# Decay factors in a PSUM bank, one PSUM bank for the attention output

## What is computed

```python
def bi_wkv(r, k, v, w, u, time_emb):          # used twice, with r = x and k = v = f
    tf = sigmoid(sum(time_emb))
    decay = exp(-exp(w)) * (0.5 + 0.5 * tf)   # per channel and batch
    ek = exp(min(k, 30)); ekv = ek * v
    # a = a * decay + ekv, b = b * decay + ek, over the 256 tokens,
    # once forward (nf, df) and once in reverse (nb, db)
    euk = exp(min(u + k, 30))
    num = nf + nb - ekv + euk * v
    den = df + db - ek + euk
    return sigmoid(r) * num / max(den, 1e-8) * (0.8 + 0.2 * tf)

x = x + attention(bi_wkv(x, f, f, w1, u1, cond))    # 16 heads of 16
x = x + moe_ffn(bi_wkv(x, f, f, w2, u2, cond))      # 64 experts, 6 used, and 2 shared tiles
```

## Time and profile before

| | before |
|---|---|
| median of 3 runs | 434.53 us (433.73 to 434.86) |
| the profiled execution's own time | 433.69 us |
| its span in the profile | 431.9 us |
| TensorE busy (matmul) | 333.6 us, 77% |
| VectorE busy | 305.9 us, 71% |
| ScalarE busy | 186.8 us, 43% |
| GpSimd busy | 140.3 us, 32% |

### The profile page before, as it was taken

The page is one execution under the profiler, slowest core; times in us unless marked ns, Lnnn a source line. Parts: engine busy times, 40 slices in busy tenths (PEclk is TensorE's granted clock), DMA queues, the critical chain, the costliest instruction groups (busy, mean ns, idle before and its releaser), DMA issues.

```text
span 431.9 us, 6069 instructions
## 1 busy us (share of the span) xinstructions
PE 333.6 (77%) x1628; PEld 261.3 (60%) x1628; DVE 305.9 (71%) x658; ACT 186.8 (43%) x373; POOL 140.3 (32%) x123
## 2 busy tenths in 40 slices
PE   0014337747876786888857999999999999999995
PEld 0013225536654675665546788888888888888884
DVE  6999988995799866777567766556565565555654
ACT  4014030535261545557352555455554555545541
POOL 2608553325223002003303443443334433344331
PEclk9998555955895798899798999999999999999999
DMA  5940390850183039010100111111011101111102
GB/s 168 176 132 24 116 151 2 198 97 2 50 187 59 3 112 172 14 50 2 51 0 0 51 49 49 49 49 38 35 49 49 49 31 42 49 49 49 30 18 97
DMA packets 16947, 28.02 MB, mean 65 GB/s; under 512 B 2418, under 2 KB 10786, under 8 KB 15906
## 3 DMA queue, kind: packets, MB, share of 16 engines
q1 hardware_dynamic: 16930, 27.82, 27.7%
HBM read 20.81 MB, written 5.24 MB: 60 GB/s over the span
## 4 chain that ended last, share of the span: by engine, by line
issue 31%; DVE 13%; POOL 10%; PE 9%; ACT 3%; DMA 2%; POOLq 1%; DVEq 1%; SPq 0%; ACTq 0%
POOL scan L418 9%; DVE scan L1075 4%; PE ps L1182 2%; DVE mx L804 2%; DMA k_st<-qk_split 1%; PE ps L1150 1%; PE ps L1169 1%; PE ps L1212 1%; PE ps L1139 1%; ACT prob L495 1%; PE ps L1223 1%; DVE hid L850 1%; DMA qk_split<-qk_lo 0%; DVE scan L736 0%; ACT o_raw L502 0%
## 5 line engine op out<-in xcount | busy, mean ns | idle before, releaser
L418 POOL TENSOR_TENSOR scan<-scan 128x512 f32<-128x512 f32 x68 | 75.4, 1111 | 131.5 <-ACT scan L556 131.5
L1075 DVE TENSOR_TENSOR scan<-scan,ps 128x512 f32<-128x512 f32 x64 | 44.0, 687 | 60.0 <-POOL scan L418 60.0
L560 ACT ACTIVATE q_st<-scan 128x512 fp32r<-128x512 f32 x64 | 40.5, 632 | 58.8 <-PE ps L1286 52.2
L1266 PE MATMUL ps<-hid_hi,k_st 128*128 128x512 f32 (+1 forms) x140 | 55.0, 393 | 2.5 <-DVE k_st L960 2.2
L1150 PE MATMUL ps<-k_st,q_st 96*128 96x256 f32 x128 | 34.8, 394 | 27.1 <-DMA k_st<-qk_split 21.7
L1079 DVE TENSOR_TENSOR q_st<-scan,q_st 128x512 fp32r<-128x512 f32 x64 | 44.1, 689 | 16.3 <-ACT q_st L560 16.3
L556 ACT ACTIVATE scan<-ps 128x512 f32<-128x512 f32 x68 | 40.4, 598 | 33.5 <-PE ps L1268 31.6
L1284 PE MATMUL ps<-q_st,k_st 128*128 128x512 f32 x136 | 54.3, 399 | 0.6 <-POOL q_st L429 0.4
L1268 PE MATMUL ps<-hid_hi,k_st 128*128 128x512 f32 (+1 forms) x140 | 54.7, 391 | 0.0
L1267 PE MATMUL ps<-hid_lo,k_st 128*128 128x512 f32 (+1 forms) x140 | 54.6, 390 | 0.0
L1285 PE MATMUL ps<-q_st,k_st 128*128 128x512 f32 x136 | 53.9, 396 | 0.0
(11 more groups left out here) (133 smaller groups left out, 542.7 us busy)
## 6 DMA issues: line engine op xcount, KB each, us to landing
clip<-in_tiles SPq DMA_DIRECT2D x34, 256.0 KB, 2.6
q_st<-qk_split SPq DMA_DIRECT2D x16, 256.0 KB, 4.8
k_st<-qk_split SPq DMA_DIRECT2D x32, 128.0 KB, 5.5
qk_split<-qk_hi SPq DMA_DIRECT2D x8, 256.0 KB, 2.1
qk_split<-qk_lo SPq DMA_DIRECT2D x8, 256.0 KB, 2.1
f_sb<-in_fT SPq DMA_DIRECT2D x4, 256.0 KB, 10.1
x_sb<-in_xT SPq DMA_DIRECT2D x4, 256.0 KB, 9.2
out<-f_sb SPq DMA_DIRECT2D x4, 256.0 KB, 2.3
```

Source lines behind the costliest of these rows:

```text
L418: g.tensor_tensor(sq[:, half], relu[:, half], relu[:, half], ALU.mult).then_inc(sq_ready, 1)
L1075: TT(act[:, half], sq[:, half], bank_w(half), ALU.mult).then_inc(act_ready, 1)
L1266: mm(bank_h(slot)[:, cols], w_hi, x_hi, start=(c == 0), stop=False)
```

## The change

`decay` is no tensor in SBUF any more but the first 16 floats of PSUM bank 5 on every partition. The attention output has only bank 4. `values` waits for ScalarE's copy of the group before it (`o_raw_ready`), where it waited for that of the group before the last.

```diff
--- before.py
+++ after.py
@@ -89,7 +89,7 @@
         cfac = sb("cfac", [P, B])
         dexp = sb("dexp", [P, 2 * KC])
         dbase = sb("dbase", [P, 2 * KC])
-        decay = sb("decay", [P, 2 * KC, B])
+        decay = ps[:, 5, 0:2 * KC * B].rearrange("p (n b) -> p n b", b=B)
 
         clip = sb("clip", [P, 4, KC, S])
         gkv = clip[:, 0:2]
@@ -209,8 +209,8 @@
         def bank_t(n):
             return ps[:, 2 + n % 2, :].rearrange("p (t q) -> p t q", t=QT)
 
-        def bank_o(n):
-            return ps[:, 4 + n % 2, 0:S]
+        def bank_o():
+            return ps[:, 4, 0:S]
 
 
         jobs = [("q", 0), ("k", 0), ("v", 0)]
@@ -499,7 +499,7 @@
                 if b > 0:
                     n = job_no[("ot", b - 1, 1)]
                     sc.wait_ge(misc_full[n % 2], n // 2 + 1)
-                a.activation(o_raw[:, grp], bank_o(4 * b + grp), ACT.Copy).then_inc(o_raw_ready, 1)
+                a.activation(o_raw[:, grp], bank_o(), ACT.Copy).then_inc(o_raw_ready, 1)
 
             def evacuate_o_ch(b):
                 job_wait(sc, ("oc", b))
@@ -1172,14 +1172,14 @@
 
             def values(b, grp):
 
-                if 4 * b + grp > 1:
-                    pe.wait_ge(o_raw_ready, 4 * b + grp - 1)
+                if 4 * b + grp > 0:
+                    pe.wait_ge(o_raw_ready, 4 * b + grp)
                 pe.wait_ge(v_ready, QT * (b + 1))
                 pe.wait_ge(prob_ready, H * b + 4 * grp + 4)
                 for kt in range(QT):
                     for j in range(4):
                         h = 4 * grp + j
-                        last = mm(bank_o(4 * b + grp)[32 * j:32 * j + 32, :], v_aug[:, b % 2, kt, h, :],
+                        last = mm(bank_o()[32 * j:32 * j + 32, :], v_aug[:, b % 2, kt, h, :],
                                   prob[:, (H * b + h) % PRING, kt, :], start=(kt == 0), stop=(kt == QT - 1))
                 last.then_inc(pv_ready, 1)
```

## The result

| | before | after |
|---|---|---|
| median | 434.69 us (433.73 to 435.44, 4 runs) | 419.72 us (416.96 to 421.15, 4 runs) |
| profiled execution, its span | 433.69, 431.9 us | 419.32, 417.5 us |
| mean granted TensorE clock | 0.893 | 0.902 |

The ratio is 0.9649, 95% interval 0.9595 to 0.9703: 3.5% faster. I had predicted 419.

A forecast was written before the change was run, and what follows sets the result against it. VectorE's scans, taking turns with GpSimd on SBUF, were taken to bound the time before the expert tiles. Relief 16.1 less bank waits 1.05 gives 15.05 us; predicted 419 us (chance 0.74), range 415.5 to 424.5 for 8 in 10.

The forecast's parts named there:

- Unheld pace 0.58, PSUM at no cost: Line 736 scans take 0.58 us each when GpSimd does not hold them; reading decay from PSUM adds zero.
- The rival that a scan from PSUM costs 0.06 to 0.12 us more: All 64 scans pay for reading PSUM, 3.8 to 7.7 us together; time 423 to 427; chance 0.08.
- The relief: VectorE's scans, in all four batches, no longer wait for GpSimd: 16.1 us gained in sum.
- Batch 0: Relief: eight scans from 8.91 and what follows gain 5.0 us. Banks: second values group 1.5 us late, hidden.
- Opening in all: Scans of batches 0 and 1 ahead of qk_lo: 5.0, 6.1 and 2.0 us, together 13.1, reaching TensorE whole.
- batch 3's last eight scans: Four scans at 126.28 gain 3.1 us, less some 0.6 for the held hid of line 850: 2.5 taken.
- the rival that something at a fixed time stops it: The opening's 13.1 us are cut, by the loads or by TensorE; half the relief, 427 us; chance 0.07.
- The banks: Values groups wait for ScalarE's copy of the group before, late in three of 15 pairs: 1.05 us, bounds 0.4 and 3.9.
- Last group: Batch 3's last group of values waits for the copy at 207.49: 0.75 us, counted in full.
- Batch 1: Second group of values, at 135.61, starts 1.6 us late; mostly absorbed behind it, 0.3 taken, at most 1.6.
- That the hold stays: Scans hold and are held as before wherever decay lies; 434.7 us, within 0.3%; chance 0.05.
- the slower case: Scans held as before and batch 1's values wait on the path: 436 to 437.6 us; chance 0.06.

The follow-up runs named there:

- the kernel with memsets: The kernel before, decay in SBUF, with GpSimd's products and sums each replaced by two memsets, for timing only: 417.73 us, ratio 0.9559.
- The bank alone: The kernel before with only one output bank, decay still in SBUF: 434.16 us against 435.44, ratio 0.9971.
- the two repeats: The changed kernel itself run again twice, unaltered, against the kernel before: 418.14 us, ratio 0.9598, and 418.19 us, ratio 0.9625.
- alternating banks: The changed kernel, but from the sixth group of values on the output alternates between banks 4 and 5: 416.40 us, ratio 0.9569 to the kernel before.

## Why the prediction was right, step by step

**Unheld pace 0.58, PSUM at no cost.** Right. Four scans take 2.41 to 2.43 us from PSUM, 2.41 from SBUF with GpSimd idle; medians are 665 and 664 ns, against 666 with decay in SBUF in the kernel with memsets. The rival that a scan from PSUM costs 0.06 to 0.12 us more is out. The access overhead that the Trainium skill gives for PSUM ("Perfetto Trace Analysis", Optimizing Scalar/DVE Operations) doesn't show in this instruction: 64 scans at 0.065 us more would have been 4.2 us, and 665 against 666 ns leaves nothing of it.

**The relief.** One statement on the way was too wide: that an instruction with only one of its tensors in SBUF is not held. It was read from one pair of line 780, and it holds for all 64 scans, but not for every operation: gpen in the last section has one tensor and is held. The kernel before already gave a hint: its four clips of line 699 (one tensor and a column of vec) take 2.14 us at 56.28, beside GpSimd's den at 56.44, and 1.14 at 31.23 with GpSimd idle. The sum doesn't suffer, since these clips take 2.14 in both kernels. Batch 0: predicted 5.0, the ninth scan moves from 18.72 to 13.41; of these 5.3, 0.17 come from an earlier start (8.74 instead of 8.91: the opening transfer landed earlier). The sums behind them did meet GpSimd's last product, 1.38 us instead of 1.26. Opening in all: predicted 13.1, measured 13.4 at qk_lo, 13.2 without the earlier start. The middle gave 0.3 where I had 0.2 + 0.3, and batch 3's last eight scans 2.6 where I had 2.5; the hid of line 850 among them is held as I said (1.19 us at 116.11, 0.72 before). All scans: predicted 16.1, the last scan moves from 134.12 to 117.82, 16.3. The opening's part reached TensorE in full, and the rival that something at a fixed time stops it is out.

**The banks.** Predicted sum 1.05. Last group: predicted 0.75. The start of the group before it moved by 15.27 us (205.49 to 190.22) and that of the last, counted by its records, by 14.53: 0.74. Batch 1: the wait of 1.6 is there (1.61), but the 0.3 that I let through was nothing: the line-1169 products behind it move by 16.29, from 141.79 to 125.50, as does the last scan. Batch 0: hidden, as said; the wait is 1.39, and the scores behind it move by 12.64 (95.60 to 82.96), as those before it do by 12.61 (88.95 to 76.34). So 0.74 in place of 1.05. The bank alone shows the same 0.74 in its profile; its ratio, with 1.0004 as its upper end, would allow 0.17, so the 0.74 rests on the profiles only.

**What I had not in the sum.** Between the last scan and the last values the gain falls from 16.3 to 15.3 us. It doesn't fall evenly: it drops, comes back, and drops again. The first drop, in TensorE's timeline of the kernel before and of the changed kernel, at the same instructions of batch 1's iteration:

```profile
147.01 0.27 PE L1158 MATMUL ps<-ident,mx 128*16 128x128 f32 x1 [1.01 <-DVE mx L804]
...
148.02 1.07 PE L1182 MATMUL ps<-prob,v_aug 128*32 128x256 f32 x16
...
149.82 0.42 PE L1182 MATMUL ps<-prob,v_aug 128*32 128x256 f32 x4
```

```profile
130.25 0.27 PE L1158 MATMUL ps<-ident,mx 128*16 128x128 f32 x1 [1.56 <-DVE mx L804]
...
131.36 1.94 PE L1182 MATMUL ps<-prob,v_aug 128*32 128x256 f32 x16
...
134.38 0.87 PE L1182 MATMUL ps<-prob,v_aug 128*32 128x256 f32 x12
```

The same 16 matmuls take 1.07 us before and 1.94 after. The windows of the two kernels around them (length, busy us of TensorE, weight loads, VectorE, ScalarE and GpSimd, granted TensorE clock):

```profile
147.00:149.80 2.80, 2.79 (x27) 1.86 (x27) 1.81 (x4) 1.25 (x3) 0.00 (x0) 1.00 0.03 6
```

```profile
127.00:130.20 3.20, 1.52 (x10) 1.07 (x8) 3.18 (x12) 1.90 (x4) 0.00 (x0) 1.00 0.00 0
130.20:134.30 4.10, 4.05 (x27) 2.40 (x27) 1.81 (x4) 1.25 (x3) 0.00 (x0) 0.60 0.02 4
```

Before, this stretch has the higher level, 2.4 GHz. After, the clock is at that level up to 130.2, while TensorE is busy for 1.52 of 3.20 us, and then falls to 0.60, mostly the lower level of 1.2 GHz. The shift is 16.76 us at the first TensorE row and 15.44 at the last. By the scores in the middle of batch 2's iteration it is back at 16.65 (line 1158, 180.75 before and 164.10 after), and right behind them the same thing happens a second time: 16 matmuls take 1.07 us at 181.75 before and 1.90 at 165.10 after, and behind them the shift is 15.3. Whether the change brings these falls each time or they are chance was not tried; in other stretches the clock is a little higher than before, and the mean is too (0.902 and 0.893).

Together, at the end of the attention: 16.3 - 1.0 - 0.74 = 14.5, and the span fell by 14.4. I had 15.05: relief 0.2 short, banks 0.3 too dear, and the clock's 1.0 missing. In the medians the difference is 14.97 us.

**How much of the match is luck.** The held scans' part repeats: qk_lo starts at 36.33, 36.35 and 36.32 in the three profiles of the changed kernel, and batch 3's last eight scans take 5.23, 5.24 and 5.24 us from the first start to the last, against 7.84 before and 7.85 with the bank alone. That is 13.4 + 2.6 = 16.0 us of relief, and the mechanism is right in it. What lies between the first scores and those eight scans does not repeat: it takes 65.7, 64.5 and 61.9 us in the three (granted clock 0.70, 0.73, 0.78), and 65.8 and 64.3 (0.71, 0.73) in the two kernels with decay in SBUF. Nor does the stretch from the shared tile's first product to the first expert tile: 25.3, 26.3 and 27.9 us (0.89, 0.80, 0.76), and 25.1 before (0.93). So two single executions can differ by up to 4 us in the first stretch alone, and in the two repeats the medians lie 17.2 and 17.5 us apart. That 15.05 meets 14.97 to a tenth is luck; that the gain lies near 16.0 less the bank waits in all three comparisons is not.

**The rivals of no gain.** That the hold stays is out by the maximum of 693 ns; the slower case with it.

## What to carry to other kernels

Compare equal instructions beside a busy and an idle GpSimd: rows that double there and nowhere else show a hold, and the distance between the two is what moving one operand can buy, where the other engines wait for them. The cheapest operand to move is the smallest, here 16 floats a partition into a PSUM bank, and the bank is found where a copy out of a double-buffered one mostly ends before the next group starts. Look then at what comes next on both engines: a wait that is removed can bring other VectorE operations beside GpSimd's reads.

## What the runs showed of the hardware

The hold strikes very short VectorE operations too, and which of them differs from one execution to the next. VectorE's timeline of the changed kernel, in the profile of the result and in its first repeat, in the router of batch 3:

```profile
214.30 1.26 DVE L894 TENSOR_TENSOR gsum<-fmax,fsec 128x16 f32<-128x16 f32 x1
...
216.41 0.17 DVE L910 TENSOR_SCALAR gpen<-grep 128x16 f32<-128x16 f32 x1
```

```profile
215.99 0.96 DVE L894 TENSOR_TENSOR gsum<-fmax,fsec 128x16 f32<-128x16 f32 x1
...
217.80 1.24 DVE L910 TENSOR_SCALAR gpen<-grep 128x16 f32<-128x16 f32 x1
```

Both long gsum start within 0.15 us behind a GpSimd operation (214.24 and 215.88), and so does the long gpen (217.72); the gpen of 0.17 us starts in the last 0.1 us of one (215.48 to 216.52). An operation of 0.17 us takes 1.24, and gpen has one SBUF tensor as input, unlike the scans, so the rule of two SBUF inputs doesn't cover it; whether it ran in one of the modes that the rule's second half excepts, no run here shows. The clips at 42.89 (2.14 us for four, 1.13 elsewhere) are of this kind too, and the hid at 52.11 (1.82 instead of 0.75) of the first.

Single executions of one kernel spread by about 1.5%, often with TensorE's granted clock: with alternating banks 414.0 us at 0.917 and 420.07 at 0.898, the changed kernel 416.78 at 0.914 and 420.88 at 0.902. Not always, though: with the scans of batches 2 and 3 in PSUM it was 431.72 at 0.905 and 431.69 at 0.893. This spread is why differences under 1 us stayed open.
